# Splitting each attention score matmul into four column groups of 32 keys

## The reference

```python
scores = einsum('bhsd,bhtd->bhst', q_embed, k_embed) / D ** 0.5      # first: positions as angles
scores = -(sq_norm - 2.0 * dot + sq_norm.T) * inv_sqrt_dk            # second: squared distances
scores = einsum('bhqd,bhkd->bhqk', q, k) / sqrt(D) + G               # third: a bias by position
attn = softmax(scores, axis=-1)
out = einsum('bhst,bhtd->bhsd', attn, v)
```

## Time and profile before

| what | value |
|---|---|
| median of 3 runs | 1988.55 us (1987.03 to 2001.31) |
| the profiled execution | 1999.54 us, span 1997.5 us, mean granted clock 0.903 |
| PE busy | 1719.4 us, 86% of the span |
| DVE busy | 1270.4 us, 64% |
| ACT busy | 1318.0 us, 66% |
| one unit in a3 and a7, in the steady part | 182.06 us for 16 units |
| one unit in a5, in the steady part | 184.56 us for 22 units |

### The profile page before, as it was taken

One profiled execution on the slowest core, in us unless ns is written; L12 is line 12 of the kernel. 1 busy time (PEld: TensorE's weight loads), 2 busy tenths in 40 slices (PEclk: granted clock), 3 DMA queues, 4 the chain that ended last, 5 costly groups with the idle time before them and its releaser, 6 DMA issues. The chain is left out here.

```text
span 1997.5 us, 30427 instructions
## 1 busy us (share of the span) xinstructions
PE 1719.4 (86%) x10142; PEld 738.7 (37%) x10142; DVE 1270.4 (64%) x2594; ACT 1318.0 (66%) x2222; POOL 350.4 (18%) x638
## 2 busy tenths in 40 slices
PE   7899966737999999888699999687653999999989
PEld 4666655521222222276122222344430222222256
DVE  4777786978999999565201111245545999999833
ACT  5555534962778787755369999475551778777853
POOL 4333214411000000043100000132311000000053
PEclk9999977966999999988569999898875999999989
DMA  4000000153222222001211111002124112212101
GB/s 113 1 1 1 1 1 1 64 180 90 66 75 72 68 78 67 17 1 40 74 35 50 51 51 43 0 17 60 41 78 121 53 54 57 59 52 61 31 6 38
DMA packets 114590, 98.48 MB, mean 49 GB/s; under 512 B 25866, under 2 KB 104516, under 8 KB 114436
## 3 DMA queue, kind: packets, MB, share of 16 engines
q1 hardware_dynamic: 112390, 95.41, 16.5%
q10 hardware_dynamic: 2046, 1.13, 0.3%
HBM read 64.34 MB, written 32.11 MB: 48 GB/s over the span
## 5 line engine op out<-in xcount | busy, mean ns | idle before, releaser
L1484 ACT ACTIVATE a_probs<-a_ps_s 128x512 f32<-128x512 f32 (+1 forms) x1280 | 803.1, 684 | 265.1 <-PE a_ps_s L1399 245.1
L1514 DVE TENSOR_REDUCE a_minus_max<-a_ps_r 128x1 f32<-128x512 f32 x1024 | 634.7, 683 | 48.4 <-PE a_ps_r L1407 48.2
L1399 PE MATMUL a_ps_s<-a_q_stack,a_k_stack 114*128 114x512 bf16 (+2 forms) x1536 | 458.0, 394 | 19.8 <-DMA a_k_stack<-n_parts 15.7
L1416 PE MATMUL a_ps_pv<-a_probs,a_v_ones 128*16 128x512 f32 x3072 | 419.9, 614 | 1.5 <-ACT a_ctxT L1475 0.7
L1407 PE MATMUL a_ps_r<-a_k_stack,a_q_stack 48*128 48x512 bf16 (+1 forms) x1024 | 200.3, 401 | 68.9 <-DMA a_q_stack<-gate_parts 34.1
L1399 PEld LDWEIGHTS a_ps_s<-a_q_stack,a_k_stack 114*128 114x128 bf16 (+2 forms) x1536 | 105.2, 98 | 382.7 <-ACT a_probs L1484 238.5
L1407 PEld LDWEIGHTS a_ps_r<-a_k_stack,a_q_stack 48*128 48x128 bf16 (+1 forms) x1024 | 59.3, 94 | 241.0 <-DVE a_minus_max L1514 127.0
L1374 POOL CAST a_max_parts<-a_minus_max 128x16 bf16<-128x16 f32 x64 | 12.6, 196 | 684.3 <-DVE a_minus_max L1514 684.3
L1530 DVE RECIPROCAL a_inv<-a_ps_r 128x16 f32<-128x16 f32 x96 | 24.8, 258 | 169.4 <-PE a_ps_r L1424 169.4
L1416 PEld LDWEIGHTS a_ps_pv<-a_probs,a_v_ones 128*16 128x16 f32 x3072 | 54.9, 95 | 144.0 <-ACT a_probs L1484 90.9
L1525 DVE COPY a_ctxT<-a_ps_pv 128x512 f32<-128x512 f32 x32 | 22.1, 692 | 130.3 <-PE a_ps_pv L1416 130.3
(11 more groups left out here) (347 smaller groups left out, 2555.5 us busy)
## 6 DMA issues: line engine op xcount, KB each, us to landing
polar_q<-d_p_q_parts SPq DMA_DIRECT2D x24, 256.0 KB, 3.0
polar_k<-d_p_k_parts SPq DMA_DIRECT2D x24, 256.0 KB, 3.2
a_q_stack<-polar_q SPq DMA_DIRECT2D x64, 96.0 KB
a_q_stack<-dist_parts SPq DMA_DIRECT2D x192, 32.0 KB
gate_parts<-d_p_curve_parts SPq DMA_DIRECT2D x24, 256.0 KB, 3.0
a_k_stack<-polar_k SPq DMA_DIRECT2D x62, 96.0 KB
a_k_stack<-dist_parts SPq DMA_DIRECT2D x186, 32.0 KB
a_q_stack<-gate_parts SPq DMA_DIRECT2D x64, 72.0 KB
```

The costliest lines, as they stand in the source:

```text
L1399: last = pe.matmul(ps_s[i % PAIRS][:, j, :], k_stack[m % SLOTS][:, h, c * P:(c + 1) * P], q_stack[m % SLOTS][:, h, :], start=True, stop=True)
L1416: last = pe.matmul(ps_pv[32 * h:32 * h + VW, :], v_ones[m % 2][:, c, h, :], probs[(NT * m + c) % PROBS][:, h, :], start=(c == 0), stop=(c ...
L1484: act.activation(probs[(NT * m + c) % PROBS][:, WIDE * part:WIDE * (part + 1), :], ps_s[i % PAIRS][:, :, :], ACT.Exp).then_inc(exp_done, 1)
L1514: dve.tensor_reduce(minus_max[n % 2][:, k:k + 1], ps[:, :], AX.X, ALU.max, negate=True).then_inc(bank_free, 1)
```

## The change

In `unit`, each score matmul becomes four. Each takes 32 of the 128 keys as weights, streams the same 512 queries, and writes 32 of the 128 PSUM partitions. The values computed, the buffers, the waits and the increments (one, on the last matmul) stay as they were.

```diff
                     for j in range(WIDE):
                         h = WIDE * part + j
-                        last = pe.matmul(ps_s[i % PAIRS][:, j, :], k_stack[m % SLOTS][:, h, c * P:(c + 1) * P], q_stack[m % SLOTS][:, h, :],
-                                         start=True, stop=True)
+                        for r in range(0, P, 32):
+                            last = pe.matmul(ps_s[i % PAIRS][r:r + 32, j, :], k_stack[m % SLOTS][:, h, c * P + r:c * P + r + 32],
+                                             q_stack[m % SLOTS][:, h, :], start=True, stop=True)
                     last.then_inc(scores_done, 1)
```

## The result

The changed kernel takes 1972.97 us (median of 4 runs, 1968.17 to 1974.51), the kernel before, with one more run beside it, 1991.89 us (1987.03 to 2001.31). The ratio is 0.9897, 95% interval 0.9864 to 0.9931: 1.0% faster, about 20 us. The forecast was 1975 us.

A forecast was written before the change was run, and what follows sets the result against it. PE was taken to bound a3, a5 and a7, with DVE 7% behind in a3 and a7. From the median 1988.55 us, -16 (a3, a7) and +3 (a5) gave 1975 us; own range 1960 to 1990, range of all 1956 to 2003.

The forecast's parts named there:

- What bounds: In a3, a5 and a7 PE sets the pace; most changes of array shape lose about 0.10 us each.
- PE's saving: In a3 and a7, two shape gaps per chunk go, one returns behind the context's transposes: 0.49 us a unit.
- The trailing quarter: The last of four score quarters trails by 0.02 us, a cost wherever a change of shape follows the scores.
- The half that DVE takes back: In a3 and a7, waiting for DVE's bank loses half of PE's saving, leaving -0.25 us a unit.
- equation of two chunks: In a3 and a7, two chunks take 2.95 us plus PE's stretch X: 2.66 us a chunk today, 2.575 after.
- The sum: Whole kernel: -16 us in a3 and a7, +3 in a5, so -13 from the median 1988.55: 1975 us.
- A: Rival: scores and products stay different shapes, the gaps stay, a3 and a7 +8, a5 +3: 2000 us; chance 0.12.
- B: Rival: a5 gains too, another -16 us, as if column groups alone decided shape: 1957 us; chance 0.10.
- C: Rival: a5 stays longer at 1.2 GHz, ten more units give 2048 us; no low stretch is -24; slow side 0.09.
- The 11 us between the profiled run and the median: Put down to a5's time at the lower clock: one and a half units more or fewer there.
- D: Rival: supply or streams limit matmuls and loads to 50 ns each, a5 at 10.0 us a unit: 2025 us; chance 0.07.

The follow-up runs named there:

- e5: The kernel before, with a3's row maxima taken over the first 256 of 512 keys only: 1973.61 us, ratio 0.9897, a unit of a3 11.09 us.
- e6: The changed kernel, with a3's row maxima taken over the first 256 of 512 keys only: 1945.91 us, ratio 0.9758, a unit of a3 10.51 us.
- e1: The changed kernel with quarters of 32 keys in a3 and a7 only, a5 keeping whole scores: 1967.37 us, ratio to before 0.9864.
- e3: The changed kernel with each score matmul as two of 64 keys instead of four of 32, in all three attentions: 1994.21 us, ratio to before 0.9999.
- e4: The changed kernel with a5's stacks padded from 54 to 72 rows, zero in the keys: 1943.62 us, ratio to before 0.9736.
- e11: The kernel before, profiled again with nothing changed: 1991.89 us, with a5 at 1.2 GHz for 25 us.
- e7: The kernel before with a5's stacks padded from 54 to 72 rows and scores left whole: 1983.07 us, ratio 0.9951.

## Why the prediction was right, and where its terms were off

**What bounds** held. PE set the pace, DVE was next, and each overlap read in the earlier trace rows told what the array would do: gaps at the two changes that went are gone, those at the tiles stayed, the one behind the transposes appeared, and a5 with 54 rows kept all of its own. Halves, and quarters in a5 without the rows, showed that splitting alone gives nothing.

**PE's saving** was mis-sized: 0.49 us a unit, where e5 and e6 measure 0.58, and 0.62 once the waits left in them are taken out. Two sizes are off. The trailing quarter, four times 0.02, doesn't show, and the gap behind the products is more than 0.10: from the start of the products over the scores to the start of the tiles, the three steps of a unit fall from 1.52, 1.49 and 1.52 us (before) to 1.40, 1.39 and 1.42, so by 0.10 to 0.12, where the gap less the trailing quarter had been put at 0.075. Scores to products fell by 0.09, and the step behind the context's transposes grew by 0.09, as forecast. In a5 the trailing quarter was priced at 0.02 a chunk, 0.08 a unit and +3 us; measured are 0.02 a unit, (134.62 - 134.22) / 16, with 134.22 us from sixteen units of e1's a5, whose scores are whole:

```profile
1060.58:1194.80 134.22, 134.22 (x836) 34.29 (x832) 19.87 (x48) 124.06 (x129) 4.71 (x16) 1.00 0.17 51
```

**The half that DVE takes back** was right: 0.33 of 0.62 us arrives, and half would be 0.31. But that the equation of two chunks gave today's 2.66 us was no test of it. Its terms are stretches of one trace that together make up two chunks, so they add up to twice 2.66 whatever holds PE up. The test is e5 and e6. The waits are also less even than the equation has them: it has one wait in every chunk, and the table of e5 and e6 shows two that went (0.13 us for POOL, 0.09 for DVE's product) and one that grew to 0.37 us.

**The sum.** 64 units x 0.33 = 21 us against 16 forecast, a5 +1 against +3, so -20 in place of -13, and the medians moved by 19 us, the ratio stands for 20. The forecast of 1975 stood 2 us from the measured 1973, since the median of before had moved from 1988.6 to 1991.9 with one more run: 7 us too little in the terms and 3 us too little in the starting point cancel in part; that it came within 2 us is luck. The forecast's range of 0 to 31 us in a3 and a7 was wide enough, and the half was worth having: with all of the 0.49 counted the forecast would have been 1960.

**The rivals.** A fell with the overlap of 0.17 us and e3 shows what it would have been. B fell with 8.41 us a unit; e4 shows that it needs the rows. C, the clock, can't be seen to move with the change: a5's low stretch is 25 to 56 us with whole scores of 54 rows and 25 to 40 with quarters. Its -24 us for no low stretch should have been -26 by its own rows, 56.30 x (1 - 8.39 / 15.66), and less for an execution near the median. The 11 us between the profiled run and the median, which the prediction put down to this stretch alone, need not all be that: e11 shows that stages before a3 move by several us too. The two profiles that the first comparison rests on, 56 and 25 us, differ by two steps, worth 14 of their 31 us; whoever had compared these two alone would have found half as much gain again as there is. D, supply, fell outright: a5 was given 1605 matmuls and 1601 loads in 134.62 us, 42 ns each, for the whole stage, and PE stayed busy throughout. Its price was also too low: at 50 ns the 236 instructions of a unit of a3 and a7 would take 11.8 us instead of 11.1, another 43 us or so, which the 2025 us leave out.

## What to carry to other kernels

Where a stream mixes matmuls of different parts of the array, read the overlap of each group's end with the next group's start: on this chip and kernel 0.17 us meant nothing lost and 0.07 meant about 0.10 us lost, and making neighbours take the same rows and columns (splitting columns, padding rows with zeros) gets it back, and in a3 and a5 it cost next to nothing in streaming. Before counting a saving on the bounding engine in full, write down the loop through the next engine's buffers; here it gave back nearly half. And compare clocks before comparing two profiles.

## What the runs showed of the hardware

- A change of shape costs about 0.10 us at 2.4 GHz: 0.09 behind scores, 0.10 to 0.12 behind products. By the overlaps, 114 and 126 rows (0.16 to 0.17 us behind the 128-row transposes, in a3 and a7 before) and 72 rows (0.16, e7) count as 128 rows, 54 do not (0.07), and 64 columns stay apart from the products' 16 (0.07, e3). 16 columns share the shape of 32 (0.17, changed kernel), although the one is f32 and the other bf16; so do the maxima's transposes and the products. **The Trainium skill**, page TensorEngine Tiling (Array Packing), Key Properties, names the drain; its price is from here.
- Four bf16 matmuls of 32 columns and 512 streamed columns run side by side as fast as one of 128: the changed kernel's a3 has eight of them in 0.62 us, where two whole ones take 0.61.
- I had not expected padding to shorten the low stretch. With PE busy throughout, a5 stayed at 1.2 GHz for 25 to 57 us in nine profiles with 54 rows, and for 5 to 8 us in four with 18 rows of zeros more. Why is not shown. The e7 runs without a profile fall near 1979 and 1987 us, 7 and 15 above the profiled one, which is the size of one and two low units; longer stretches with padding alone would explain it, and so, in part, would the stages before a3. No profile of a slower one was taken, and this stays open.
